# A state-space layer and a gathered expert layer on one core: the weighed rows of a group move from among the dots of the second next group to among the dots of the next

## What is computed

```python
x = _layernorm(x + attn(x))          # in-projection, 4-tap convolution, state-space scan, gate, out-projection
h = silu(x @ W_up.T + b_up) @ W_down.T + b_down            # 512 -> 2048 -> 256
q = h @ W_q.T                                              # 8 heads, two halves
scores, idx = top_k(q . keys, 8)                           # two lists of 8 per head
sc, pk = top_k(all 64 sums of pairs, 8)                    # 8 of 4096 experts per head
de, ue = down_embed[indices], up_embed[indices]            # 64 rows per token
z = silu((h . de) * softmax(sc))
x = _layernorm(x + sum over the 64 of z * ue)
```

## Time and profile before

| | us |
|---|---|
| median of 3 runs | 3161.11 (3151.85 to 3166.98) |
| the profiled execution | 3151.04 |
| its span on the core | 3149.2 |
| busy: PE / DVE / ACT / POOL | 2790.8 / 2777.5 / 2049.7 / 2062.7 |
| DVE: dots (2048) / weighed rows (1376) | 823.8 / 1040.6 |
| DVE idle for gathered rows / for the convolution's inputs | 136.1 / 102.5 |

### The profile page before, as it was taken

The page is one execution under the profiler, slowest core; times in us unless marked ns, Lnnn a source line. Parts: engine busy times, 40 slices in busy tenths (PEclk is TensorE's granted clock), DMA queues, the critical chain, the costliest instruction groups (busy, mean ns, idle before and its releaser), DMA issues.

```text
span 3149.2 us, 44785 instructions
## 1 busy us (share of the span) xinstructions
PE 2790.8 (89%) x11776; PEld 1737.3 (55%) x11776; DVE 2777.5 (88%) x10160; ACT 2049.7 (65%) x6513; POOL 2062.7 (65%) x2056
## 2 busy tenths in 40 slices
PE   7989899998898999999899989899898999898863
PEld 4565456655555655555566545556555565555541
DVE  3489899998899999999899989999999999899986
ACT  3466766666776666676666676666676666677642
POOL 0066666676676667666667666666766666766676
PEclk9999999999999999999999999999999999999986
DMA  8088888888888888888888888888888888888888
GB/s 284 23 263 275 270 279 273 277 290 282 272 285 265 270 292 287 276 282 277 265 277 297 273 276 271 273 278 290 284 277 268 276 272 288 283 278 281 277 303 272
DMA packets 189855, 856.76 MB, mean 272 GB/s; under 512 B 36192, under 2 KB 39392, under 8 KB 189088
## 3 DMA queue, kind: packets, MB, share of 16 engines
q0 software_dynamic: 163840, 805.44, 77.0%
q1 hardware_dynamic: 19104, 34.87, 3.2%
q10 hardware_dynamic: 6656, 13.60, 1.2%
HBM read 845.38 MB, written 8.39 MB: 271 GB/s over the span
## 4 chain that ended last, share of the span: by engine, by line
PE 38%; DVE 32%; DMA 9%; POOL 9%; issue 7%; ACT 5%; POOLq 0%; SPq 0%; DVEq 0%; ACTq 0%
DVE bank L1143 14%; POOL ring L276 9%; DMA ring<-embed,idx 9%; PE bank L500 8%; DVE ring L1129 8%; PE bank L359 7%; DVE xc L974 6%; PE bank L339 5%; PE bank L441 4%; PE bank L488 4%; PE bank L368 3%; ACT xc L679 1%; PE bank L376 1%; PE bank L307 1%; ACT xskip L691 1%
## 5 line engine op out<-in xcount | busy, mean ns | idle before, releaser
L276 POOL DMA_INDIRECT ring<-embed,idx x2048 | 2061.4, 1007 | 1074.8 <-issue 532.3
L1143 DVE SCALAR_TENSOR_TENSOR bank<-ring,coef,bank 128x512 f32<-128x512 f32 x1312 | 992.4, 756 | 7.4 <-issue 0.2
L1129 DVE SCALAR_TENSOR_TENSOR ring<-ring,hcur 128x256 f32<-128x256 f32 x2048 | 823.8, 423 | 138.5 <-DMA ring<-embed,idx 136.1
L645 ACT ACTIVATE coef<-prob,zp 128x1 f32<-128x1 f32 x2048 | 456.0, 286 | 630.8 <-DVE ring L1129 625.4
L500 PE MATMUL bank<-ring,diag_c 128*128 128x512 f32 x1344 | 672.8, 631 | 115.9 <-ACT diag_c L654 101.3
L463 PE MATMUL bank<-zs,w_up 128*128 128x128 f32 x4096 | 502.2, 287 | 69.2 <-ACT zs L767 65.8
L463 PEld LDWEIGHTS bank<-zs,w_up 128*128 128x128 f32 x4096 | 496.2, 203 | 110.2 <-ACT zs L767 91.8
L500 PEld LDWEIGHTS bank<-ring,diag_c 128*128 128x128 f32 x1344 | 247.2, 199 | 379.2 <-issue 223.7
L974 DVE SCALAR_TENSOR_TENSOR xc<-raw,taps,xc 128x128 f32<-128x128 f32 x960 | 266.2, 351 | 102.6 <-ACT xc L679 102.5
L339 PE MATMUL bank<-w_in,ut 128*128 128x512 f32 (+1 forms) x768 | 285.8, 524 | 4.0 <-ACT seg L667 3.9
L654 ACT ACTIVATE diag_c<-cst,coef 128x128 f32<-128x128 f32 x672 | 234.8, 394 | 48.4 <-PE bank L500 38.0
(11 more groups left out here) (144 smaller groups left out, 3422.2 us busy)
## 6 DMA issues: line engine op xcount, KB each, us to landing
ring<-embed,idx POOLq DMA_INDIRECT x2048, 4.6
ring<-uT SPq DMA_DIRECT2D x4, 2048.0 KB, 14.2
ut<-uT SPq DMA_DIRECT2D x32, 256.0 KB, 6.5
zs<-u SPq DMA_DIRECT2D x32, 256.0 KB, 5.6
out<-acc SPq DMA_DIRECT2D x32, 256.0 KB, 4.6
w_up<-W_upT ACTq DMA_DIRECT2D x1, 4096.0 KB, 13.0
w_in<-W_in ACTq DMA_DIRECT2D x1, 2560.0 KB, 17.4
w_in<-W_in ACTq DMA_DIRECT2D x1, 2048.0 KB, 22.0
```

The source lines that it names most:

```text
L276: pool.indirect_dma_start(out=ring[:, k % RING, :], out_offset=None, in_=embed, in_offset=bass.IndirectOffsetOnAxis(ap=idx[:, half, k:k + ...
L645: m = act.activation(coef[:, k:k + 1], prob_v[:, k:k + 1], ACT.Silu, scale=zp[:, k:k + 1])
L1129: m = dve.scalar_tensor_tensor(out=ring[:, k % RING, 0:DP], in0=ring[:, k % RING, 0:DP], scalar=1.0, in1=hcur[:, :], op0=ALU.mult, op1=ALU ...
L1143: dve.scalar_tensor_tensor(out=total if n == len(DVE_ROWS) - 1 else running[:, :], in0=ring[:, k % RING, DP:ROW], scalar=coef[:, k:k + 1], ...
```

## The change

`LAG` becomes 1. Nothing else is edited. The same 2048 dots and 1376 weighed rows are issued, with the same operands; the streams of ACT, PE, POOL and SP stay as they are, and on DVE the weighed rows stand one group earlier. `weigh_all` keeps only the rows of the last group.

```diff
 NEW = 4
-LAG = 2
+LAG = 1
 NGRP = len(GROUPS)
```

## The result

| | us |
|---|---|
| kernel before, median of 4 runs | 3159.94 (3151.85 to 3166.98) |
| kernel after, median of 4 runs | 3394.86 (3390.81 to 3399.07) |
| ratio, with its 95% interval | 1.0744 [1.0715, 1.0774] |
| span of the profiled execution, before / after | 3149.2 / 3393.5 |

The change makes the kernel slower by 235 us; the forecast was +174 on the median (3335), in a range up to 3390. The sign and most of the mechanism were right, and 60 us are missing in it.

A forecast was written before the change was run, and what follows sets the result against it. A chain of touching links across PE, ACT and DVE, not one engine, was taken to bound each tile; 2.5 + 2.8 + 0.6 = 5.9 us over some 30 tiles gave +177 us, predicted 3335, range 3235 to 3390.

The forecast's parts named there:

- A: Front of the tile, gate to convolution: waits for ACT's coefficients delay the in-projection's copy and PE's third part, +2.5 us a tile.
- B: From the convolution to h: three more weighed rows and a wait for coefficients in group 11, +2.8 us a tile.
- C: End of the tile: weighed rows ahead of the last dots delay ACT's coefficients and those dots, +0.6 us a tile.
- D: Ring slots of D rows come free one group earlier, which could speed gathers: put at 0 us a tile.
- third rival: Ring was the limit: earlier free slots remove DVE's waits for gathers, so the kernel gets faster, 3092 us; chance 0.06.
- Rival 2: Delays feed each other through ACT's later work, which PE waits for: 7.8 us a tile, 3385 to 3400 us; chance 0.12.

The follow-up runs named there:

- e4: Kernel before, with weighed rows one group behind their dots in groups 13 to 17 only: 3153.6 us, ratio 0.9989.
- e1: Kernel before, with weighed rows one group behind their dots in groups 1 to 4 only: 3275.2 us, ratio 1.0378.
- e2: Kernel before, with weighed rows one group behind in groups 6 to 12 only (group 6 takes those of 4 and 5): 3326.9 us, ratio 1.0539.
- e3: Kernel before, with weighed rows one group behind from group 18 on (18 takes those of 16 and 17): 3176.3 us, ratio 1.0066.
- e18: Kernel after, with weighed rows of group 2 back in group 4 and those of 3 and 4 in group 5: 3314.0 us, ratio 1.0484.
- e17: Kernel after, with four matmuls that nothing reads put on PE ahead of its wait for h: 3328.8 us, ratio 1.0538.
- e8: Kernel before, with the second matmul of `state_in` issued four times to fill PE's wait for the gate: ratio 1.0058, on a chip with gaps.
- e11: Kernel before, with the weighed row of group 4 moved to group 5: ratio 0.9979, on a chip with gaps.

## Why the prediction was right, and where it was wrong

**What bounds the kernel**: right. DVE from the convolution to h and PE behind it are on the path; e4 shows that the same move is free outside of it, and e1, e2 and e3 each pass their delay on to the period.

**A, forecast 2.5**: right in its size, with luck in two of its steps. The last dot of group 4 and ACT's first copy are 2.34 us later (forecast 2.4 for the dot), the residual 1.57 (forecast 1.6), and in e18, which takes A away, the convolution is back to +0.15. The first slip is in the count of rows: up to the first dot of group 3 there are five weighed rows in both kernels, not one fewer. That dot is earlier all the same, by 0.97 us (forecast 0.66), because DVE's waits for gathers in groups 1 and 2 went from 1.13 us a tile to 0.14. It did not matter, since ACT ends the coefficients of group 2 12.2 us behind the gate in both. The second slip is the end of PE's first two parts, put at 1034.8 by taking 2/3 of 8.59. The third part is only half as wide as the others, and ACT's timeline shows PE releasing the second copy at 1035.96:

```profile
1035.96 0.60 ACT L667 ACTIVATE seg<-bank 128x512 f32<-128x512 f32 x1 [1.02 <-PE bank L339]
```

So in the tile that was read the first copy had about 1 us of slack. On the mean of the tiles it has none (it ends 20.25 us behind the gate, the third part starts at 20.44 behind a wait of 0.15), and the conclusion held.

**B, forecast 2.8**: 5.83 - 2.97 = 2.86. Right.

**C, forecast 0.6**: 8.09 - 7.41 = 0.68. Right; the row of group 20 is the one that waits, 1.55 us in the tile shown. Alone, in e3, the same stretch grew by 1.8 us.

**D, forecast 0**: near it in after, but no run tests it by itself. DVE waits 65 us less for gathers; 1.0 us a tile of that lies ahead of group 3, where DVE then waits for ACT instead. In e3, which has no such wait for ACT, earlier gathers give some 0.8 us a tile back. The third rival's 3092 is out by 300 us. The Trainium skill's "Perfetto Trace Analysis", section "Optimization Strategy", says that a gap which repeats on the engine that should be saturated can mean too few buffers, a condition that the forecast left out; POOL, 61% busy in after, is no such engine, and its gaps for PE's rows grew to 561.3 us while DVE's waits for gathers halved.

**The failing step** is the one between h and C: "The third stretch begins with h, later by A + B", with everything behind it at the length that it had in the earlier trace rows. The sum added waits ahead of the keys and of the in-projection's third part and had no term for these matmuls themselves: it left the in-projection at its 8.59 us, and the keys at what they took in the tile that was read. Behind these waits PE ran part of its matmuls at the lower clock level, 1.2 GHz in place of 2.4: +1.6 us a tile in transposes and keys and +0.6 at the third part and the transposes behind it (2.97 at the convolution less the 2.34 of ACT's copy). 5.9 and 2.2 are 8.1 a tile, and 8.12 was measured. e17 bears the sum out as well: with the clock held up at h the tile costs 5.74 us more than before, against 5.9 forecast (before has 0.3 us a tile of slow keys of its own, which e17 has not).

The trace of before had the row that would have told it. In five of its tiles the wait for h was 2.2 to 2.9 us and the starts of the eight key matmuls spanned 4.5 us and more, where they span 3.0 in the others; a change forecast to add 2.7 us to that wait in every tile had to be priced with the slow keys, not with those of a tile in which PE had waited 0.57. The chance was not certain, for six other tiles waited 2.2 us and kept the full clock.

**Rival 2** (delays feed each other, 3385 to 3400) has the measured time, 3394.9, and not the cause. It asked for A 2.7, B 3.6 and C 1.5; measured were 2.3 (2.97 with the slower third part), 2.9 and 0.7, and e17 removes the excess on PE with ACT's delays all in place.

**What would show it**: the wait at L1143, 177.7 us or 5.6 a tile, came as forecast; DVE's wait for the convolution's inputs was to go towards 150 and went to 154.9; PE's wait for h was to grow by 80 and grew by 85; the gathers' wait was to fall well below 136.1 and fell to 71.1; the stretches of the tile were to become 28 and 30 and became 28.85 and 29.92. All five held, and none of them looked behind h, where the error was.

## What to carry to other kernels

When an edit makes PE wait longer for another engine, price the matmuls behind the wait too: look in the trace for a tile in which PE already waits that long, read the granted clock and the duration there, and take those in place of the usual ones. A step that stands on the path costs its own time however idle its engine looks on the page, and the same step a few instructions further, behind the one that others wait for, costs nothing (e2 and e4). Before choosing how far a consumer runs behind its producer, look at when the producer's answer is ready at each place; here one distance served for the whole tile, and a few of its 22 places made all of the loss.

## What the runs showed of the hardware

**PE's clock behind waits.** PE's granted clock fell behind waits of 2.2 to 5 us that repeat once a tile; behind those of 0.6 us in before and of 1.5 us in e17 the keys were never slow. The mean clock of after is 0.939 and of before 0.953; at two levels, 1.0 and 0.5, that is (1 - 0.939) x 2 x 3393.5 = 414 us at the lower level against 296. In e17 it is 260, with more matmuls. A wait of a given length does not settle it: behind 2.2 us the keys of before were slow in four tiles and at full speed in six others, those of e1 slow in two of 18, and after's transposes of y ran at 1.00 behind a wait of 3.19 (windows of the wait and of what follows):

```profile
1186.70:1189.91 3.21, 0.03 (x1) 0.00 (x0) 3.21 (x7) 3.18 (x14) 2.60 (x3) 1.00 0.97 333
1189.91:1197.00 7.09, 6.91 (x22) 3.45 (x23) 6.59 (x21) 4.31 (x17) 5.26 (x7) 1.00 0.91 313
```

So the price of a wait is a share of tiles times 1.5 us or so. It does not simply grow with the wait: in after the keys lost 1.5 us on the mean behind waits of 3.5 us and 1.1 behind 4.95, and in e2, behind 4.3, they lost 0.8. The Trainium skill, "TensorE: Matmul & The Clock Gate", section "HAM oscillation — how this bites in real kernels", says that a wait which repeats in a loop sends the matmuls behind it back to the lower clock each time; this trace agrees in kind, for waits on another engine where the page has waits for DMAs, and e17 puts the cost here at 60 to 70 us of 3160, 2%.

**Matmuls nobody reads can pay.** e17's 256 extra matmul instructions cost nothing, because they lie in a wait, and gave 2% of the changed kernel. In the kernel before the wait for h is mostly too short for it (0.57 us in the earlier trace rows's tile), and it was not tried there on a chip without gaps. Over half of the time at the lower level within a tile of before, 3.5 of 6.5 us, lies behind the gate, and e8, the one run that filled the wait there, gained nothing.

**Chips differ.** Two chips stood apart. The same kernel took 3157 to 3163 us on the other chips and 3639 to 3645 on these two, where PE stood idle in the up-projection for causes that the profile does not name. Of e11, which is nearly the kernel before, the waits list has:

```profile
PE bank L463 <- issue: 105.1, 154, 4.1
```

In before, on another chip, this is a single wait of 3.4 us. A ratio to the kernel before on the same chip did not make the runs comparable: the effect under study was covered there.
